# Second-phase constants and head products moved into the last quad of a Mamba, cross-attention and LoRA-expert layer; last layer norm cut into the slots of sequence 0

## What is computed

```python
x = _layernorm(x + attn_ref(x, ...))       # Mamba: in_proj, conv, selective scan, gate, W_out
x = _layernorm(x + xattn_ref(x, ctx, ctx, Wq, Wk, Wv, Wo, bo, g))   # linear cross-attention, 8 heads
x = _layernorm(x + ffn_ref(x, router_w, A, B))     # top-2 of 4 LoRA experts

# inside xattn_ref, per sequence
qh = softmax(Wq q, over the 64 channels of a head) * SCALE
kh = softmax(Wk k, over the positions)
context = einsum('bhdn,bhen->bhde', kh, vh)
out = einsum('bhde,bhdn->bhen', context, qh);  out = Wo out + bo
```

## Time and profile before

| | |
|---|---|
| median of 3 runs | 3032.15 us (3032.04 to 3032.88) |
| profiled execution, its own time | 3033.12 us |
| its span, first to last instruction | 3031.0 us |
| mean granted TensorE clock | 0.959 of full |
| busy: PE, DVE, ACT, POOL | 2745.5, 2552.6, 1693.4, 1926.4 us |
| first phase ends (last gate product on DVE) | 2220.7 us from the start |

### The profile page before, as it was taken

One profiled execution on the slowest core, in us unless ns is written; L12 is line 12 of the kernel. 1 busy time (PEld: TensorE's weight loads), 2 busy tenths in 40 slices (PEclk: granted clock), 3 DMA queues, 4 the chain that ended last, 5 costly groups with the idle time before them and its releaser, 6 DMA issues.

```text
span 3031.0 us, 35275 instructions
## 1 busy us (share of the span) xinstructions
PE 2745.5 (91%) x11120; PEld 1568.1 (52%) x11120; DVE 2552.6 (84%) x3522; ACT 1693.4 (56%) x2846; POOL 1926.4 (64%) x884
## 2 busy tenths in 40 slices
PE   8968899999989999998999888898878999999996
PEld 4535555555555555555555444555444555555553
DVE  2359999999999999999999999999936787777775
ACT  2347566565665657556565565665605555555553
POOL 1159897888969889797898987988802222222221
PEclk9989899999999999999999998898889999999998
DMA  5432333424343344334333322322121111111110
GB/s 171 135 100 80 99 98 106 138 87 131 87 155 106 93 128 126 107 94 143 115 94 98 94 86 85 119 85 77 42 70 70 62 55 55 62 62 54 56 62 21
DMA packets 132876, 281.32 MB, mean 93 GB/s; under 512 B 12528, under 2 KB 12656, under 8 KB 132224
## 3 DMA queue, kind: packets, MB, share of 16 engines
q1 hardware_dynamic: 132736, 279.59, 29.6%
HBM read 245.86 MB, written 33.69 MB: 92 GB/s over the span
## 4 chain that ended last, share of the span: by engine, by line
PE 55%; DVE 31%; issue 9%; ACT 4%; POOL 1%; DMA 0%; DVEq 0%; SPq 0%; ACTq 0%; POOLq 0%
DVE arena L1216 17%; PE banks L454 15%; PE banks L478 9%; DVE arena L1232 7%; PE banks L536 7%; PE banks L629 4%; PE banks L672 4%; PE banks L585 3%; PE banks L610 3%; PE banks L491 2%; PE banks L640 2%; PE banks L600 2%; ACT banks L981 1%; DVE arena L1172 1%; PE banks L679 1%
## 5 line engine op out<-in xcount | busy, mean ns | idle before, releaser
L1142 POOL TENSOR_TENSOR arena<-arena 128x2048 f32<-128x2048 f32 x256 | 1162.3, 4540 | 78.7 <-PE banks L536 78.5
L1216 DVE TENSOR_TENSOR_SCAN arena<-banks,arena 128x512 f32<-128x512 f32 x1024 | 1185.1, 1204 | 20.0 <-POOL arena L1142 16.8
L981 ACT ACTIVATE banks<-arena,a_sb 128x508 f32<-128x508 f32 x1024 | 696.9, 684 | 735.2 <-DVE arena L1216 734.7
L454 PE MATMUL banks<-arena 128*128 128x512 f32 x2048 | 955.8, 604 | 11.6 <-DMA arena<-in_xT 8.7
L536 PEld LDWEIGHTS banks<-ident,arena 128*128 128x128 f32 x4096 | 493.5, 146 | 418.9 <-issue 197.0
L536 PE MATMUL banks<-ident,arena 128*128 128x128 f32 x4096 | 576.5, 284 | 137.3 <-DVE arena L1232 68.9
L454 PEld LDWEIGHTS banks<-arena 128*128 128x128 f32 x2048 | 374.1, 195 | 365.4 <-issue 362.2
L1232 DVE SCALAR_TENSOR_TENSOR arena<-banks,cg,arena 128x512 f32<-128x512 f32 x640 | 452.9, 738 | 71.6 <-PE banks L536 70.9
L478 PE MATMUL banks<-arena 128*128 128x512 f32 x1024 | 473.0, 601 | 3.0 <-DVE arena L1336 3.0
L1088 POOL TENSOR_TENSOR arena<-arena 128x512 f32<-128x512 f32 x240 | 306.2, 1276 | 204.1 <-ACT arena L811 201.8
L1153 POOL TENSOR_TENSOR arena<-arena 128x512 f32<-128x512 f32 x128 | 141.3, 1104 | 462.8 <-DVE arena L1382 462.8
(11 more groups left out here) (137 smaller groups left out, 2979.2 us busy)
## 6 DMA issues: line engine op xcount, KB each, us to landing
arena<-b_scratch SPq DMA_DIRECT2D x128, 512.0 KB, 5.1
arena<-in_WinX SPq DMA_DIRECT2D x128, 256.0 KB, 2.8
arena<-in_WinZ SPq DMA_DIRECT2D x128, 256.0 KB, 2.7
arena<-in_WoutT SPq DMA_DIRECT2D x32, 1024.0 KB, 5.3
u_scratch<-arena SPq DMA_DIRECT2D x64, 256.0 KB, 5.1
arena<-u_scratch SPq DMA_DIRECT2D x16, 1024.0 KB, 9.5
arena<-x_scratch SPq DMA_DIRECT2D x32, 512.0 KB, 3.5
arena<-in_xT SPq DMA_DIRECT2D x14, 1024.0 KB, 8.0
```

Of the source, the lines that this page charges most:

```text
L454: last = nc.tensor.matmul(home(kind, i), wr[w % 2][:, k, :], x[:, k, :], start=(k == 0), stop=(k == KC - 1))
L981: nc.scalar.activation(by_seq(bank(i % 2))[:, :, 1:SEQ], by_seq(dt[s % 2][:, i, :])[:, :, 1:SEQ], ACT.Exp, scale=a_sb[:, QD * q + i, n:n + ...
L1142: nc.gpsimd.tensor_tensor(hb[n % 4].rearrange("p (i t) -> p i t", i=QD), dtu, brep[pair % 3][:, n % 2:n % 2 + 1, :].broadcast_to([P, QD, G ...
L1216: nc.vector.tensor_tensor_scan(h, bank(i % 2), h, 0.0, ALU.mult, ALU.add)\
```

## The change

1. The buffers of the second phase get other places in `arena`, so that the constants, the head weights, the context and the input of sequence 0 lie in buffers that the last quad doesn't use.
2. `sync_second`, called once in the last quad after its sixth broadcast of B, loads all of them (eleven DMAs).
3. The head products become two jobs "P" of four matmuls in the places that X2 and X3 leave empty in the last quad's list; `act_heads` copies them on ACT at e = 54 and e = 63 in place of the DVE copy.
4. After the last quad PE starts with key tile 0 and then does two output products after each key tile, in place of four output products, the head products, and one output product after each key tile.
5. The last layer norm is spread: DVE takes the statistics of one sequence at the end of slots 0 to 3 of sequence 0, the power is on POOL ahead of its slot 4, the shift on DVE in slot 6, and ACT applies one of the four at the start of each of slots 7 to 10.

`sync_wo` is not touched.

```diff
+FREED = {..., "P": "ph_ok"}
 def job(s, name):
+    if kind == "X" and s + 1 == NS and i > 1:
+        return "P", i - 2
...
+        def sync_second(sp):
+            sp.wait_ge(S["x_mm"], NG * DT)
+            sp.dma_start(wvh[0:DH], a["Wvh"]).then_inc(S["wv_loaded"], 16)
+            sp.dma_start(woh[0:DH], a["Woh"]).then_inc(S["wv_loaded"], 16)
+            sp.dma_start(cn, a["ctx"][0]).then_inc(S["cn_loaded"], 16)
+            sp.dma_start(cT, a["ctxT"][0]).then_inc(S["ct_loaded"], 16)
+            sp.wait_ge(S["ss_mm"], NG * DT // 2)
+            sp.wait_ge(S["fin"], QD * (NS - 1))
+            for dst, name in consts2:
+                sp.dma_start(dst, a[name]).then_inc(S["p2_const"], 16)
+            sp.wait_ge(S["x1_stored"], 16 * (NG - 1))
+            sp.dma_start(x1, x1_d[0]).then_inc(S["x1_loaded"], 16)
...
             sync_b(sp, s, 5)
+            if s == NS - 1:
+                sync_second(sp)
...
+        def pe_heads(pe, j):
+            pe_room(pe, "P", j)
+            pe.wait_ge(S["wv_loaded"], 32)
+            for h in range(4 * j, 4 * j + 4):
+                last = nc.tensor.matmul(home("P", j)[:, h % 4 * P:(h % 4 + 1) * P], wvh[0:DH, h, :],
+                                        woh[0:DH, h, :], start=True, stop=True)
+            last.then_inc(S["ph_mm"], 1)
...
+            if s == NS - 1 and e in (54, 63):
+                act_heads(act, (54, 63).index(e))
...
 # act_sequence, in slot t
+                if opening and t >= SLOTS - GB:
+                    act_ln_apply(act, NG - 1, t - SLOTS + GB)
...
 # pool_sequence, in slot t
+                if opening and t == 4:
+                    pool_rstd(pool, NG - 1)
...
 # dve_sequence, at the end of slot t
+                if opening and t < GB:
+                    dve_ln_tile(dve, NG - 1, t)
+                if opening and t == 3:
+                    dve_ln_spread(dve, NG - 1)
+                if opening and t == 6:
+                    dve_ln_shift(dve, NG - 1)
...
 # SP, after the last quad
             sp.wait_ge(S["fin"], QD * NS)
-            sp.wait_ge(S["x1_stored"], 16 * (NG - 1))
-            for dst, name in consts2:
-                sp.dma_start(dst, a[name]).then_inc(S["p2_const"], 16)
-            sync_context(sp, 0)
-            for b in range(2):
-                sync_seq(sp, b)
+            sync_seq(sp, 0, opening=True)
+            sync_seq(sp, 1)
...
 # PE, after the last quad
-            for c in range(4):
-                for k in range(QD):
-                    pe_out(pe, 8 * (NS - 1) + c, k)
             pe.wait_ge(S["p2_const"], C2)
-            for h in range(HEADS):
-                last = nc.tensor.matmul(bank(h // 4)[...], wvh[0:DH, h, :], woh[0:DH, h, :], ...)
-            last.then_inc(S["ph_mm"], 1)
             for o in range(OT):
                 pe_keys(pe, 0, o)
-                for k in range(QD):
-                    pe_out(pe, 8 * (NS - 1) + 4 + o, k)
+                for c in (2 * o, 2 * o + 1):
+                    for k in range(QD):
+                        pe_out(pe, 8 * (NS - 1) + c, k)
```

More of the change, by code:

```diff
@@ L67 @@
 SPACE = 100
-FREED = {"X": "conv_done", "Z": "z_exp", "O": "r_added", "D": "dt_ok", "Y": "fin"}
+FREED = {"X": "conv_done", "Z": "z_exp", "O": "r_added", "D": "dt_ok", "Y": "fin", "P": "ph_ok"}
 def has_x(s):
@@ L419, in sync_context, with sync_seq @@
                 .then_inc(S["cn_loaded"], 16)
-        def sync_seq(sp, b, store=None, context=True):
+        def sync_seq(sp, b, opening=False, store=None, context=True):
             row = x1_d[bass.ds(b, 1)].rearrange("a p h -> (a p) h")
-            sp.wait_ge(S["q_mm"], 8 * b)
-            sp.dma_start(x1, row).then_inc(S["x1_loaded"], 16)
-            sp.wait_ge(S["g_mm"], b)
-            sp.dma_start(cT, a["ctxT"][bass.ds(b, 1)].rearrange("a p n c -> (a p) n c"))\
-                .then_inc(S["ct_loaded"], 16)
+            if not opening:
+                sp.wait_ge(S["q_mm"], 8 * b)
+                sp.dma_start(x1, row).then_inc(S["x1_loaded"], 16)
+                sp.wait_ge(S["g_mm"], b)
+                sp.dma_start(cT, a["ctxT"][bass.ds(b, 1)].rearrange("a p n c -> (a p) n c"))\
+                    .then_inc(S["ct_loaded"], 16)
             if store is not None:
@@ L510, in pe_filler @@
                         kind, i = found
-                        if kind == "D":
+                        if kind == "P":
+                            if k == 0:
+                                pe_heads(pe, i)
+                        elif kind == "D":
                             pe_dt(pe, i)
@@ L799, in act_ln_apply, with act_heads @@
                                  scale=ve1[:, t:t + 1]).then_inc(S["ln_ok"], 1)
+        def act_heads(act, j):
+            act.wait_ge(S["ph_mm"], j + 1)
+            act.wait_ge(S["ss_mm"], NG * DT // 2)
+            nc.scalar.activation(ph[:, 4 * j:4 * j + 4, :], home("P", j).rearrange("p (h c) -> p h c", h=4), ACT.Copy)\
+                .then_inc(S["ph_ok"], 1)
         def act_part(act, s, n):
@@ L1245, in dve_out, with dve_ln_tile, dve_ln_spread @@
             nc.vector.tensor_tensor(v, home("O", i), v, ALU.add).then_inc(S["r_added"], 1)
+        def dve_ln_tile(dve, g, t):
+            dve.wait_ge(S["r_added"], 8 * NQ * (g + 1))
+            for h in range(2):
+                nc.vector.bn_stats(st1[:, t, h, :], rbuf[:, t, h * HALF:(h + 1) * HALF])\
+                    .then_inc(S["ln_stats"], 1)
         def dve_ln_stats(dve, g):
[L1248 removed]
             for t in range(GB):
[L1250 to L1252 removed]
+                dve_ln_tile(dve, g, t)
+            dve_ln_spread(dve, g)
+        def dve_ln_spread(dve, g):
             dve.wait_ge(S["ln_stats"], 8 * g + 8)
@@ L1620, in _ @@
                 act_keys(act, 0, o)
-            act_sequence(act, 0, keys=True, tail=False)
-            for t in range(GB):
-                act_ln_apply(act, NG - 1, t)
+            act_sequence(act, 0, keys=True, tail=False, opening=True)
             with nc.scalar.Fori(1, BATCH - 1) as b:
```

110 lines of the change are left out of this document (49 added, 61 removed).

## The result

The changed kernel took 3011.96 us (median of 4 runs, 3009.90 to 3013.76), the kernel before beside it 3032.43 (4 runs, 3032.04 to 3032.88): ratio 0.9934, 95% interval 0.9921 to 0.9946. Predicted were 3013.3, with a range of 3006 to 3020.

The account below looks back on a forecast made before the run. It took a chain of waits through TensorE and VectorE as the bound, with one long transfer wait at the seam. Gains 15.9 + 3.5 - 0.5 = 18.9 us gave 3014.2, or 3013.3 at the median; range 3006 to 3020.

Parts of the forecast that it names:

- The last quad, 0.5 predicted: Last quad: the second ACT copy of head products, ahead of state 13's application, costs 0.5 us, between 0 and 0.67.
- DVE sets the pace there, so I count no gain: Last quad: the second head-product group shortens a 2.13 us TensorE wait that dropped the clock; gain counted as none.
- the rival of a late broadcast: Last quad: the 3.2 MB burst delays the broadcast for states 10 and 11, making the kernel slower; chance 0.03.
- The seam, 43.8 predicted: From the last quad's last turn to the first query product: 43.8 us against 59.65, gain 15.9.
- The first gap: Behind the last turn: key tile 0 fills 1.72 of 3.05 us, 1.3 stay idle, clock taken as full.
- The wait for the weights: Seam, ahead of the fifth output product: TensorE waits 3.7 us for the second half, landing taken as 5.4.
- The low clock behind: Seam, output products behind the wait for weights: TensorE's lower clock costs 3.0 us.
- Sequences 0 and 1, 49.9 predicted: First query product of sequence 0 to the fourth of sequence 1: 49.9 us against 53.40, gain 3.5.
- the 7.4 that the lump had cost: Layer norm in one piece between sequences 0 and 1: 20.38 us against an undisturbed 12.95, 7.4 us to win.
- a wait of 2 us or more costs about 3 us behind it: TensorE anywhere: idle of 2 us or more lowers the clock, costing about 3 us; 1.7 us didn't.
- 1.0 to 1.6 us, below those that dropped the clock: Sequence 0 with the spread layer norm: TensorE's single waits come out at 1.0 to 1.6 us, below those that dropped the clock.
- my 3.5: Sequences 0 and 1: the spread layer norm gains 3.5 us, 4 of the lump's 7.4 being given back.

Follow-up runs that it names:

- the spread alone: The kernel before with only the spread of the last layer norm, seam untouched: 3027.82 us, ratio 0.9983.
- the early second half: Changed kernel with the second half of the last quad's output weights asked for ahead of the first, right after the input projections: 3006.83 us, ratio 0.9915.
- both halves the first time: Changed kernel with both halves of the last output weights asked for together, in the old order, after the eighth output product: 3005.31 us; run again, 3006.21.
- the lump put back: Changed kernel with the last layer norm back in one piece between sequences 0 and 1, seam's change kept: 3016.44 us, ratio 0.9945.
- the early weights: Changed kernel with the second half of the last output weights asked for early, alone (3006.83 us) or together with the first half (3005.31 us).

## Why the prediction was right

**The last quad, 0.5 predicted, about 0 measured.** The price of the copy was right: ahead of the part it costs 0.48 to 0.49. TensorE's waits at these turns went as said too: the 2.13 us became 1.05 (2192.54), with no low clock behind. The wrong step is "DVE sets the pace there, so I count no gain". In the kernel before, DVE waits 0.19 us for the first of the turns at the lower clock and needs 1.60 for the two weightings; in the changed kernel it doesn't wait and needs 1.40 (DVE's timeline, before and after):

```profile
2193.26 1.60 DVE L1232 SCALAR_TENSOR_TENSOR arena<-banks,cg,arena 128x512 f32<-128x512 f32 x2 [0.19 <-PE banks L536]
```

```profile
2193.22 1.40 DVE L1275 SCALAR_TENSOR_TENSOR arena<-banks,cg,arena 128x512 f32<-128x512 f32 x2
```

The two turns take 2195.17 - 2192.54 = 2.63 us to the next output product, where they took 2195.82 - 2192.31 = 3.51. ACT's exponentials, which wait for the scans, show the gain: up to the one at 2193.95 they start 0.23 us later than in the kernel before (2193.72), from the next one on 0.24 us earlier (2195.78 against 2196.02). This step of 0.47 to 0.48 is in all twelve profiles that have the head products in the last quad, and not in that of the spread alone. So the kept clock gave back what the copy cost. The 0.24 by which the last turn ended later was there ahead of both. The term of 0.5 in the sum should have been nothing. No wait shows that the eleven transfers cost anything, and the rival of a late broadcast is gone with that.

**The seam, 43.8 predicted, 44.16 measured.** The first gap, the key tile in it and the kept clock were right to the hundredth: the first output product starts 3.05 us behind the last turn. The wait for the weights was right in place and cause, since it goes when they are asked for early. Its size was 0.6 too small: 4.26 for 3.7, because I took 5.4 us for the load to land and it took 5.81. The low clock behind was 0.4 too dear, 2.56 for 3.0, and the wait for the last residual sum 1.26 for 1.09. The Trainium skill's formula ("DMA: Bandwidth & Descriptors", section "Anatomy of one DMA", estimate 4.4 us for this megabyte) would have made the landing 1.4 us too short; the measured landing decides. The Trainium skill gives that formula for transfers that GpSimd issues, which the prediction leaves out; SyncE issues these, so the difference doesn't speak against it.

**Sequences 0 and 1, 49.9 predicted, 49.47 measured.** The landmarks came as worked out, each a little early: second key product 15.33 (15.7), last key product 30.61 (31.0), first key turn 36.52 (37.0). The causes are shown by moving them: 1.87 us for the statistics and 1.64 for the applications, together 3.5 of the 7.4 that the lump had cost; I had put 4.0 for the two. The 1.16 for an application was right as a delay: its row shows 1.24, but the instruction behind it starts 1.13 us after it (2291.51 - 2290.38), since rows overlap by about 0.1.

**What was wrong in the working.** The sentence that a wait of 2 us or more costs about 3 us behind it, and one of 1.7 nothing, is no rule. Its price was off: behind the 2.13 us the two turns lost 0.9 us of TensorE's time (3.51 for 2.63 in the changed kernel), and at the seam the wait for the weights cost 2.6 us behind it in one profile and 1.8 in another. Nor does 2 us divide the waits. The stretch of code in the last sequence loses 1.7 us behind a wait of 2.02 in nine profiles and nothing in four. And in three profiles (the early second half, both halves the first time, the lump put back) two output products of the last quad take 5.29 or 5.30 us behind waits of 1.46 and 0.46 us, with a granted clock of 0.56 to 0.57 in their first 3 us, where they take 3.60 in the nine others with the head products there. One program, both halves early, has both cases:

```profile
2197.14 5.29 PE L502 MATMUL banks<-arena 128*128 128x512 f32 x8
```

```profile
2199.67 3.60 PE L502 MATMUL banks<-arena 128*128 128x512 f32 x8
```

The kernel before and the one with the spread alone wait 0.99 and 1.00 us there and take 3.60; whether the change brought this loss, two profiles can't say. So "1.0 to 1.6 us, below those that dropped the clock" was no safe bound for sequence 0, and that none of its waits dropped the clock was partly luck. The prediction's sum is touched as well: 1.00 of the 7.4 us that I took as the lump's was the length of one low stretch in one execution. That my 3.5 nevertheless came so near to 3.93 owes something to luck.

**The scatter** of 2 to 3 us that these kernels show has two sources that the profiles name: the place in the last sequence (1.7 us) and that in the last quad (1.7 us). They met with opposite signs in two profiles of the early weights, where the last quad lost it and the last sequence didn't. The position of the last turn moves by more than that, from 2216.67 to 2219.05 over the profiles. ACT's exponentials lie up to 1.8 us earlier and 0.9 later than in the kernel before at 2110 already, and no run tested why. That the scatter comes from the low clock at the seam was an idea that fell: the kernels without that stretch scatter as much (3004.54 to 3007.32).

## What to carry to other kernels

When a long wait is removed, look for transfers that were issued while it lasted and are ordered behind work of the same stretch: they are the next wait, and their price is issue to landing less the work that is left to cover it, plus the clock. A small piece of work that is moved onto busy engines is best placed by what stands behind it there: the same layer norm cost 3.5 us ahead of a key maximum and a key exponential, and 0.03 us in waits of 2.0 to 2.7 us that DVE had anyway. And before a difference of 1 or 2 us between two profiles is put down to an edit, compare the durations of the same matmuls and the granted clock behind their waits: if these differ, more executions are needed.

## What was not expected of the hardware

Behind one and the same wait the granted clock fell in some executions of a program and not in others: 2.02 to 2.03 us of idle TensorE ahead of the query turn in the last sequence, in thirteen profiles, with 1.7 us lost behind it in nine.

The fall can also come later than the wait, which is easy to misread. In the kernel before:

```profile
2177.72 1.26 PE L536 MATMUL banks<-ident,arena 128*128 128x128 f32 x8 [2.32 <-DVE arena L1232]
2178.82 3.58 PE L454 MATMUL banks<-arena 128*128 128x512 f32 x4
```

The turn behind this wait runs at full speed, but the two matmuls behind the turn take 3.58 us, where the same two take 1.88 elsewhere (2187.42): the granted clock is 0.93 from 2178 to 2179 and 0.50 from 2179 to 2182. So a wait is done with only when what stands a few us behind it has been looked at.

How long the lower level lasts differs as well: behind a wait of 4.68 to 4.69 us the same four matmuls of the attended product took 5.29 in one and 4.30 in another. The Trainium skill ("TensorE: Matmul & The Clock Gate", section "What's actually happening") says that the number of matmuls at the lower clock at a kernel's start differs from run to run of one kernel; the rows here agree in kind, and show it in the middle of a kernel too.

Matmuls without a use, five in a wait of 4.3 us and two in one of 2.0, left no low clock behind them in the one profile that each has. The two cost no time, since a wait of 0.31 us is left behind them; the five cost about 0.3 us at most, by the estimate above.
